# Grouped attention of a four-layer network: from phases per key head to a pipeline of half-group steps, and banded queries spread on GpSimd

## The reference, cut to what matters

```
H, KV, D = (16, 4, 128)                    # 16 query heads, 4 key/value heads
q, gate = jnp.split(qg, 2, axis=-1)
q = _layernorm(q, q_norm_w, q_norm_b);  k = _layernorm(k, k_norm_w, k_norm_b)
# _rope: out = stack([xr * c - xi * s, xr * s + xi * c])
q = _rope(q, cos, sin);  k = _rope(k, cos, sin)
scores = einsum('bhqd,bhkd->bhqk', q, k) / sqrt(D)    # causal mask, softmax
out = einsum('bhqk,bhkd->bhqd', attn, v)
out = out * jax.nn.sigmoid(gate)
return out @ w_o.T
```

## Time and profile before

| what | value |
|---|---|
| median of 3 runs | 2183.93 us (2183.38 to 2186.18) |
| the profiled execution, own time | 2181.16 us |
| its span | 2179.9 us |
| instructions | 17492 |
| PE, DVE, ACT, POOL busy in the span | 1703.0, 1348.0, 800.9, 387.1 us |
| mean granted TensorE clock | 0.862 of 2.4 GHz |

### The profile page before, as it was taken

How to read it: one execution, slowest core, us unless ns; L and a number is a source line. 1 busy time by engine, 2 the same in 40 slices (tenths; PEclk the granted TensorE clock), 3 DMA queues, 4 the chain that set the end, 5 groups by cost and what they waited for, 6 DMA issues and landing times.

```text
span 2179.9 us, 17492 instructions
## 1 busy us (share of the span) xinstructions
PE 1703.0 (78%) x5814; PEld 948.5 (44%) x5814; DVE 1348.0 (62%) x2300; ACT 800.9 (37%) x1445; POOL 387.1 (18%) x261
## 2 busy tenths in 40 slices
PE   0699888877879999977887978764567777659999
PEld 0265444445643434335445453542222332226777
DVE  8474456454425636459486675876576898944565
ACT  4312434243322212243343453432354363313453
POOL 5000033110000101011020200100013765502332
PEclk9965899976759999998989989876577999969999
DMA  2000266150030000010000001000100000020110
GB/s 80 0 1 1 75 247 229 61 116 20 1 118 0 0 0 0 0 56 12 10 25 11 24 1 49 1 1 1 41 0 0 0 1 0 0 63 29 54 50 28
DMA packets 35839, 76.73 MB, mean 35 GB/s; under 512 B 5442, under 2 KB 22804, under 8 KB 33190
## 3 DMA queue, kind: packets, MB, share of 16 engines
q1 hardware_dynamic: 30662, 49.92, 7.3%
q0 software_dynamic: 5088, 25.69, 3.4%
HBM read 67.34 MB, written 7.21 MB: 34 GB/s over the span
## 4 chain that ended last, share of the span: by engine, by line
PE 56%; DVE 25%; issue 8%; ACT 6%; POOL 2%; PEldq 1%; DMA 1%; PEld 0%; SPq 0%; POOLq 0%; DVEq 0%; ACTq 0%
PE bank L157 41%; PE bank L2254 2%; PE bank L532 2%; PE bank L546 2%; PE bank L1215 2%; DVE g_q L1553 2%; PEldq L145 1%; DVE s_bu L2066 1%; POOL s_bu L2170 1%; DVE s_bu L2058 1%; DVE g_p L1577 1%; PE bank L1442 1%; DVE g_rs L1551 1%; DVE g_q L1543 1%; DVE g_p L1563 1%
## 5 line engine op out<-in xcount | busy, mean ns | idle before, releaser
L2170 POOL TENSOR_TENSOR s_bu<-s_rep,s_du 128x1024 f32<-128x1024 f32 x64 | 151.4, 2369 | 355.6 <-DVE s_du L2050 242.2
L2058 DVE TENSOR_TENSOR_SCAN s_bu<-bank,s_bu 128x1024 f32<-128x1024 f32 x64 | 145.8, 2279 | 22.9 <-ACT bank L2132 12.2
L2254 PE MATMUL bank<-s_bu,ident 128*128 128x512 f32 x256 | 133.6, 649 | 1.0 <-DVE s_dl L2007 0.3
L157 PE MATMUL bank<-e_xs,e_wsp 128*128 128x512 f32 x528 | 128.1, 391 | 0.0
L1646 POOL TENSOR_TENSOR g_q<-g_rs,g_rc 128x512 f32<-128x512 f32 x40 | 52.2, 1305 | 426.7 <-DVE g_rs L1545 426.7
L2132 ACT ACTIVATE bank<-s_dl,s_an 128x510 f32<-128x510 f32 x128 | 83.0, 682 | 106.1 <-DVE s_bu L2058 106.0
L157 PE MATMUL bank<-r_am,r_b 128*128 128x512 f32 x240 | 109.7, 597 | 0.0
L157 PEld LDWEIGHTS bank<-e_xs,e_wsp 128*128 128x128 f32 x528 | 99.1, 188 | 21.8 <-ACT e_cf L2444 0.7
L157 PE MATMUL bank<-conditioned,g_wqk 128*128 128x512 f32 x160 | 84.0, 656 | 21.6 <-DVE g_wqk L1530 21.6
L1406 POOL TENSOR_TENSOR r_ys<-r_y,r_y 128x512 f32<-128x512 f32 x14 | 22.8, 1631 | 433.7 <-DVE r_y L1351 433.7
L1633 ACT ACTIVATE g_p<-g_p,g_st 128x128 f32<-128x128 f32 (+1 forms) x128 | 57.2, 447 | 97.3 <-DVE g_st L1580 97.3
(11 more groups left out here) (458 smaller groups left out, 3981.1 us busy)
## 6 DMA issues: line engine op xcount, KB each, us to landing
e_wgu<-in_e_gu SPq DMA_DIRECT2D x22, 256.0 KB, 2.7
b_vw<-b_values SPq DMA_DIRECT2D x48, 64.0 KB, 3.1
e_wd<-in_e_down SPq DMA_DIRECT2D x22, 128.0 KB, 2.6
r_w<-in_r_w SPq DMA_DIRECT2D x3, 896.0 KB, 7.9
g_wqk<-in_g_qk SPq DMA_DIRECT2D x4, 640.0 KB, 4.1
g_wgv<-in_g_gv SPq DMA_DIRECT2D x4, 640.0 KB, 3.9
g_wo<-in_g_wo SPq DMA_DIRECT2D x4, 512.0 KB, 3.5
m_sorted<-m_zero SPq DMA_DIRECT2D x1, 1920.0 KB, 12.4
```

What stands on the lines that cost most here:

```text
L157: last = e.matmul(out, lhs, rhs, start=start and n == 0, stop=stop and n == len(pairs) - 1, skip_group_check=True)
L2058: e.tensor_tensor_scan(b, flat(k.pairs[n % 2][:, :, :]), b, 0.0, ALU.mult, ALU.add).then_inc(k["s_scanned"].up(), 1)
L2170: e.tensor_tensor(m.bu[n % m.NBU][:, :, :], m.rep[:, 2 * np:2 * np + 2, :], m.du[:, et, half(h)].unsqueeze(1).to_broadcast([P, 2, HALF]), ...
L2254: summed = e.matmul(banks[6][:, :], k.ident[:, :], m.bu[(n - 1) % m.NBU][:, i, :], start=np == 0 and i == 0, stop=np == m.NP - 1 and i == ...
```

## The change

**Grouped attention** becomes a software pipeline. A step is one half (512 tokens) of one group, so there are 8. A pass has 8 slots; in pass n, step n is projected, normalised and turned ("new"), step n-1 has its scores, softmax and first batch's values ("now"), and step n-2 its second batch's values, its gate and its output product ("old"). There are 10 passes. Each engine's list is written slot by slot. Besides, four units are transposed together, key tile by key tile, so that copies and value products are 512 columns wide; the product with `rot` is gone: DVE multiplies each half of the channels by the sine from 64 partitions to the other 64; scale and shift (`affine`) move from DVE to ACT; the variance is copied out by an Identity on ACT and Ln and Exp run on three and then on two heads, each pair with two table loads. The background takes two steps per slot. Bank 7 is shared by the values of the new step and the outputs of the old one. The first query and key weights are loaded before the tables.

**Banded attention**: ACT copies each later query projection from PSUM to `b_qs`, POOL writes the twelve later blocks from there, and the projections of the second half stand at n = 2, 4, 6, 8 of the loop rather than at 3, 6, 7, 10.

```
+def grouped_rope(k, e, f, j):
+    e.wait_ge(*k["g_affine"].at(n + 1))
+    e.tensor_tensor(both(turn[0:64, :]), both(m.rs[64:P, j, :]), table(m.rsn[64:P, :]), ALU.mult).then_inc(k.v_steps.sem, 1)
+    e.tensor_tensor(both(turn[64:P, :]), both(m.rs[0:64, j, :]), table(m.rsn[0:64, :]), ALU.mult).then_inc(k.v_steps.sem, 1)
+    e.wait_ge(*k["g_cos"].at(n + 1))
+    e.tensor_tensor(o, o, turn[:, :], ALU.add).then_inc(k["g_roped"].up(), 1)
...
+def grouped_vector(k, e):
+    for n in range(m.PASSES):
+        new, now, old = grouped_pieces(m, n)
+        for s in range(m.UNITS):
+            if now is not None:
+                grouped_greatest(k, e, now, s)
+            if s and now is not None:
+                grouped_normal(k, e, now, s - 1)
+            if s == 0 and old is not None:
+                grouped_normal(k, e, old, m.UNITS - 1)
+                grouped_gate(k, e, old, 0, 1)
+            if now is not None and s in (0, 1, 2):
+                grouped_rope(k, e, now, 2 + s)
+            if now is not None and s == 0:
+                grouped_scale(k, e, now, 4)
+            if s in (2, 4) and old is not None:
+                grouped_gate(k, e, old, 1, s // 2 - 1)
+            if s == 6 and now is not None:
+                grouped_gate(k, e, now, 0, 0)
+            if s in (6, 7) and old is not None:
...
+                grouped_add(k, e, old, s - 6)
+            if new is not None:
+                if s < 5:
+                    grouped_copy(k, e, new, s)
+                if s == 5:
+                    grouped_scale(k, e, new, 0)
+                    grouped_scale(k, e, new, 1)
+                if s == 6:
+                    grouped_scale(k, e, new, 2)
+                    grouped_rope(k, e, new, 0)
+                if s == 7:
+                    grouped_rope(k, e, new, 1)
+                    grouped_scale(k, e, new, 3)
+                    if n % 2 and n // 2 + 1 < m.KV:
+                        grouped_centre(k, e, n // 2 + 1)
+                step(background, 2)
...
+def grouped_root(k, e, f, first, last):
+    e.wait_ge(*k["g_variance"].at(5 * f + last))
+    e.activation(rs, rs, ACT.Ln).then_inc(k.a_steps.sem, 1)
+    e.activation(rs, rs, ACT.Exp, scale=-0.5).then_inc(k["g_root"].up(), 1)
...
+def grouped_sums(k, e, f, j):
+    e.wait_ge(*k["g_square"].at(n + 1))
+    if n:
+        e.wait_ge(*k["g_variance"].at(n))
...
+def grouped_mix(k, e, a, b, j):
+    e.wait_ge(*k["g_turned_out"].at(n + 1))
+    e.wait_ge(*k["g_values_out"].at(a + 1))
+    if j < 2 and 4 * a + 2 * b + j:
+        e.wait_ge(*k["g_gated"].at(4 * a + 2 * b + j))
...
+def grouped_output(k, e, l, c):
+    e.wait_ge(*k["g_gated"].at(4 * l + 4))
+    if c:
+        e.wait_ge(*k["g_added"].at(2 * l + 1))
+    else:
+        e.wait_ge(*k["g_values_out"].at(min(l + 3, m.STEPS)))
...
+def grouped_tensor(k, e):
+            turn = grouped_turn(s, new, now, old)
+            if now is not None:
+                grouped_scores(k, e, now, s)
+            if turn is not None:
+                grouped_transpose(k, e, *turn)
+            if new is not None:
+                if s < 5:
+                    grouped_project(k, e, new, s)
+                if s == 4:
+                    grouped_project_values(k, e, new)
+            if s in (5, 6) and old is not None:
+                grouped_output(k, e, old, s - 5)
+            if new is not None and s > 5:
+                grouped_project_gate(k, e, new, 2 * s - 12)
+                grouped_project_gate(k, e, new, 2 * s - 11)
+            if turn is not None:
+                grouped_mix(k, e, *turn)
+            if new is not None and 1 <= s <= 5:
+                grouped_sums(k, e, new, s - 1)
...
+def banded_queries(k, e, n, bank):
+    e.wait_ge(*k["b_q"].at(n + 1))
+    e.copy(m.qs[:, :], bank[:, :]).then_inc(k["b_queries"].up(), 1)
```

More of the change, by code:

```diff
@@ L1000, in banded_sync, with banded_blocks @@
                     e.dma_start(to[:, 4 * t:4 * t + 4, :], rows).then_inc(k[f"load_b_v{b}"].up(16), 16)
-def banded_blocks(k, e, n, bank):
+def banded_blocks(k, e, n, queries, done):
     m = k.banded
@@ new lines, in grouped_turn, with grouped_centre @@
+def grouped_turn(s, new, now, old):
+    if 1 <= s <= 3 and old is not None:
+        return old, 1, s - 1
+    if 5 <= s <= 7 and now is not None:
+        return now, 0, s - 5
+    return None
+def grouped_centre(k, e, g):
+    m, D = k.grouped, k.grouped.D
+    heads = m.wqk[:, :, :].rearrange("p c (h d) -> p (c h) d", d=D)
+    e.wait_ge(*k["load_g_qk"].at(16 * (g + 1)))
+    e.reduce_sum(m.mean[:, :], heads, AX).then_inc(k.v_steps.sem, 1)
+    e.wait_ge(k.v_steps.sem, k.v_tick())
+    e.tensor_scalar(m.mean[:, :], m.mean[:, :], 1.0 / D, None, ALU.mult).then_inc(k.v_steps.sem, 1)
+    e.wait_ge(k.v_steps.sem, k.v_tick())
+    e.tensor_tensor(heads, heads, m.mean[:, :].unsqueeze(2).to_broadcast([P, CT * (m.R + 1), D]), ALU.subtract).then_inc(k["g_centred"].up(), 1)
@@ new lines, in grouped_exp, with grouped_turned_out @@
+def grouped_exp(k, e, a, u):
+    m, n = k.grouped, 8 * a + u
+    s, c = m.pp[u], 2 * u
+    e.wait_ge(*k["g_shift"].at(n + 1))
+    for i, cols in enumerate((slice(0, P), slice(P, m.W))):
+        e.activation(s[:, cols], s[:, cols], ACT.Exp, bias=m.st[:, 0, c + i:c + i + 1], scale=m.SC,
+                     accum_out=m.st[:, 1, c + i:c + i + 1]).then_inc(k["g_exp"].up(), 1)
+def grouped_turned_out(k, e, a, b, j):
+    m, n = k.grouped, 6 * a + 3 * b + j
+    e.wait_ge(*k["g_turned"].at(n + 1))
+    if n >= 2:
+        e.wait_ge(*k["g_mixed"].at(n - 1))
+    e.copy(m.pt[n % 2][:, :], k.banks[5][:, :]).then_inc(k["g_turned_out"].up(), 1)
@@ new lines, in grouped_tanh, with grouped_values @@
+def grouped_tanh(k, e, f, i):
+    m = k.grouped
+    e.wait_ge(*k["g_gate"].at(4 * f + i + 1))
+    if f >= 2:
+        e.wait_ge(*k["g_down"].at(2 * f - 2))
+    e.activation(m.th[f % 2][:, i, :], k.banks[(9 * f + 5 + i) % 2][:, :], ACT.Tanh, scale=0.5).then_inc(k["g_tanh"].up(), 1)
+def grouped_values(k, e, f):
+    m = k.grouped
+    e.wait_ge(*k["g_value"].at(f + 1))
+    if f >= 2:
+        e.wait_ge(*k["g_mixed"].at(6 * f - 6))
+    e.copy(m.v[f % 2][:, :], k.banks[7][:, :]).then_inc(k["g_values_out"].up(), 1)
```

456 lines of the change are left out of this document (224 added, 232 removed).

## The result

| | before | after |
|---|---|---|
| median | 2183.65 us (2183.11 to 2186.18) | 2218.39 us (2215.83 to 2224.23) |
| ratio to before | 1 | 1.0161 (95%: 1.0139 to 1.0182) |
| span of the profiled execution | 2179.9 us | 2223.0 us |

The changed kernel is 35 us slower. 2173 was forecast, with a range of 2135 to 2212. The profiled execution was the slowest of the four, 2224.2 us, so its stages add up to some 6 us more than the median shows.

The account below looks back on a forecast made before the run. In grouped attention the chain from slot to slot was taken as the bound, no engine. From 2181.2 us, +1.7 for grouped and -13.0 for banded attention gave 2169.9; 2.8 for median over profile made 2173, range 2135 to 2212.

Parts of the forecast that it names:

- The banded part: Banded loop: gains of 19 us less 6 for POOL's products delaying normalisations, net -13 us, between +5 and -27.
- clock term: Grouped pass: PE's 6.2 us idle in slot 5 lowers its clock; 2.0 us a pass, bounds 0 and 3.4.
- Rival 2: Grouped slots 5 and 6: idle time leaves PE at the lower clock; +36 us, 2209; chance 0.18.
- the length of the chain: Middle grouped pass: waits and work from slot to slot sum to 59.5 us, 63.5 with POOL and clock.
- T(7) to T(1): From PE's start of slot 7's scores to slot 1's in the next pass: 12.5 us, set by DVE.
- T(4) to T(6): From PE's start of slot 4's scores to slot 6's: 17.4 us, set by ACT with its three-head root.
- The POOL term: Grouped pass: POOL's cosine products delay DVE by 2.0 us a pass, bounds 0 and 5 x 1.27.
- the 55 named as a sign: End of grouped stage: drain forecast at 48 us; longer than 55 us would show the forecast wrong.
- the 0.8 named as another: Grouped stage: a granted clock under 0.8 would show the forecast wrong.
- No engine is the bound; the chain decides: Grouped pass: DVE 43, PE 41, ACT 34 us of work, all under 63.7; the slot-to-slot chain sets the time.
- rival 1: Grouped pass: the root is covered, the chain falls to 57 us a pass, 2133 us; chance 0.26.
- Rival 4: DVE's turns: half products changing partitions wait for the one before, 0.08 us each; +7, 2180; chance 0.04.

Follow-up runs that it names:

- e1: The kernel before with the banded part of the change alone; 2166.08 us, ratio 0.9918.
- e13: The changed kernel timed and profiled once more, nothing altered; 2219.39 us, ratio 1.0177.
- e14: Second timing of the changed kernel with extra PE products that alter no result, placed where PE waits in slots 0, 2, 5 and 6; 2196.82 us, ratio 1.0066.
- e15: The changed kernel with POOL's cosine products cut from 512 to 16 columns; 2223.25 us, ratio 1.0174.
- e10: e9 with the root of heads 3 and 4 behind the last tanh of slot 7, their scales and affine in the next slot 0; 2144.31 us.
- e5: The changed kernel with ACT's values copy ahead of the root, DVE's adds and gate earlier in their slots, ACT's last two tanh before Exp; 2143.35 us.
- e9: e6 with ACT's square and variance copy of a slot ahead of its copy of transposed units and Exp; 2120.26 us, ratio 0.9719.
- e8: The changed kernel with each half product writing the partitions it reads, so the turn is left out and the output differs; 2206.56 us, ratio 1.0122.
- e3: The changed kernel with ACT's copy of the values moved ahead of the root of three heads; 2189.92 us, ratio 1.0038.
- e6: e5 with the three-head root last in ACT's slot 5, slot 0's gate behind the turn of head 2, the weights' mean in slot 6; 2141.11 us.
- e2: First timing of the changed kernel with extra PE products that alter no result, where PE waits in slots 0, 2, 5 and 6; 2200.47 us, ratio 1.0076.

## Why the prediction was wrong

**The banded part**: right, with a gain on the high side. -13 was forecast; the loop shows -12.5 in the changed kernel and -17.2 in e1, whose whole time fell by 18, and PE's waits for blocks and keys are gone. The costs were both set too high: POOL's products took 2.00 us, not 2.37, and the normalisation's mean rose from 0.69 to 0.88, 3 us for sixteen rather than the 6 taken.

**Work and place of the waits**: right. In the seven passes of e13 DVE is busy 42.5 us a pass, for 43 forecast, and ACT 35.3, for 34. PE's longest wait in a pass lies where it was put, in slot 5 for the copy of the values: 6.5 us in the mean of six, for 6.2.

**The first step that failed is the clock term**: "the idle time of 6.2 us in slot 5 ... bounds 0 and two such falls, 3.4; I take 2.0". It counted one place. The trace has four in a pass, and the clock fell behind idle times of 2.45 us as behind 7.5; e14 measured 22 to 29 us over six passes, 3.7 to 4.9 a pass, above even the upper bound. Rival 2 named this mechanism and its sign, but for slot 5 alone, and took it for a lesser chance; that its 2209 lies near 2218 is in part luck, since the chain makes up the rest.

**The second is the length of the chain**, above all its step "T(7) to T(1), 12.5 us, on DVE". With PE kept at the higher level (e14) the intervals are 6.7, 13.2, 18.5, 11.5, 15.3: sum 65.3 against 59.5. Of the 5.8, 2.8 are T(7) to T(1). There PE's first projection waits for ACT's tanh of slot 0, a wait for which the forecast had no term; in the changed kernel this projection, and not DVE's turn, set T(1) in all four middle passes. By pass it is 12.1 us in e14, 16.2 with the mean of the next weights (3.75 us on DVE, where 3.1 were taken), 14.6 with one of ACT's Ln and Exp pairs for the scans, and 18.6 with both; the forecast had these pairs only ahead of a root. T(4) to T(6) is 17.8 without such a pair, for 17.4 forecast, and 20.6 with one.

**The POOL term**, 2.0 a pass, was nothing that e15 could show here, and 1 us a collision where the order moved it on the chain (e10). So the middle pass adds up: 59.5, 5.8 more chain (some 0.7 of it for the pair ahead of a root, which the forecast counted apart), 5.2 for the clock and nothing for POOL make the 70.5 measured, where 59.5, 2.0 and 2.0 made 63.5. That the POOL term was too high hid part of the two that were too low.

**Where the loss lies**, against the forecast, in the profiled execution: first stretch +2, second pass +7.8, four middle passes +28, two late ones +12.9, drain +7.2, less 4 for jobs counted apart: 54. The experiments explain the middle passes; that the others have the same causes is likely and not shown, and the second pass, which has extra products only at its very end, is as long in e14 (58.4). The drain, with 55.2 against 48, was over the 55 named as a sign; the granted clock stayed above the 0.8 named as another, since that bound was set too low to tell.

**"No engine is the bound; the chain decides"** was right, and is why the cure was in the order: rival 1 (57 a pass) is what e5 and e9 reach, once ACT's copies leave ahead of the root. The sentence "the order on ACT is fixed" was true of that kernel only. **Rival 4** had its mechanism right, at 0.11 us instead of 0.08 each (e8); at most 1.7 us a pass hang on it.

What stays open: how the chain's 5.8 us split between the held half products, the mean, the pairs and what the extra products of e14 push themselves; and how much of e8's 12 us is clock.

## What to carry to other kernels

In a software pipeline follow the lists of all engines slot by slot, and price each of PE's waits twice: for its length, and for the products behind it, which ran up to twice as long here. A long operation that needs tables (a root, 5.5 us) goes behind the small copies that other engines wait for, and must itself lie beside PE's longest stretch; after each move read the trace again, since e3, e6 and e10 each turned one wait into another. That extra products make a kernel faster is a cheap test whether the clock is part of a loss.

## What the runs showed that was not expected

- The clock fell behind idle times as short as 2.45 us (eight records in 5.37 us at a granted 0.68, and in 5.28 at 0.69 in e2 behind 2.23 us of idle time right after twelve extra products), yet not always: behind 2.23 us, with the same twelve products ahead, they took 3.67 at 1.00 in e14. The same order of instructions gives either, and the time varies with it: 461.8 and 468.8 us for the same stretch of the changed kernel, 112.2 to 117.0 for the same banded loop.
- A half product of DVE that starts in other partitions than the instruction before it (of 0.69 us) starts 0.71 to 0.72 us after it, and 0.60 where it starts in the same.
- POOL's product of 128x1024 took 2.00 us for the blocks, with both operands repeated, where the other one of that size, with one repeated, took 2.37; what makes the difference was not tried.
